# Expert weights of a Mamba and mixture-of-experts layer: one run of memory per partition and transfer, and down weights in two transfers

## The reference, cut to what matters

```
xn = layernorm(x)                                    # [2048, 512]
out = x + mamba(xn) + moe(xn) + shared(xn)

# mamba: in_proj to 2 x 1024 channels, a causal convolution of 4 taps, x_proj to dt, B and C,
#        a scan over 2048 tokens with 16 states per channel, gate, out_proj
# moe:   64 experts, 6 per token, at most 64 tokens per expert
buf = xn gathered by expert                          # [64, 64, 512]
g = einsum('ech,ehi->eci', buf, w_gate)              # w_gate, w_up: [64, 512, 352]
u = einsum('ech,ehi->eci', buf, w_up)
y = einsum('eci,eih->ech', silu(g) * u, w_down)      # w_down: [64, 352, 512]
# each y is weighted by its score and added to its token
# shared: the same form with 704 hidden channels, for all tokens
```

## Time and profile before

| what | value |
|---|---|
| time, 3 runs | 1358.88, 1363.42, 1363.46 us; median 1363.42 |
| profiled execution: span from first to last instruction | 1386.3 us |
| profiled execution: time around the span | none is given; the span is all that the profile shows of it |
| TensorE / VectorE / ScalarE / GpSimd busy | 1291.9 / 1095.9 / 910.5 / 878.1 us |
| DMA moved | 304.82 MB in 129710 packets, mean 220 GB/s |
| w_gate, w_up | 32 transfers each of 1408 KB |
| w_down | 66 transfers of 512 KB and 33 of 384 KB |

### The profile page before, as it was taken

How to read it: one execution, slowest core, us unless ns; L and a number is a source line. 1 busy time by engine, 2 the same in 40 slices (tenths; PEclk the granted TensorE clock), 3 DMA queues, 4 the chain that set the end, 5 groups by cost and what they waited for, 6 DMA issues and landing times.

```text
span 1386.3 us, 53429 instructions
## 1 busy us (share of the span) xinstructions
PE 1291.9 (93%) x21591; PEld 808.3 (58%) x21591; DVE 1095.9 (79%) x1257; ACT 910.5 (66%) x1914; POOL 878.1 (63%) x522
## 2 busy tenths in 40 slices
PE   4999989699999999999999999999999899999998
PEld 3767767445555545555555555545554577787876
DVE  4798989878988889888888898888898655646554
ACT  3756567478788788887887888777777343434343
POOL 2455448268888988988889889889898421303030
PEclk9999999789999999999999999999999999999999
DMA  8153534859898998998989989989889761313130
GB/s 289 65 224 118 218 120 172 272 170 297 257 295 274 283 269 257 304 280 248 306 259 279 288 248 308 285 252 290 263 255 300 243 231 51 132 45 137 37 144 30
DMA packets 129710, 304.82 MB, mean 220 GB/s; under 512 B 18512, under 2 KB 20304, under 8 KB 127824
## 3 DMA queue, kind: packets, MB, share of 16 engines
q1 hardware_dynamic: 122048, 285.13, 63.3%
q0 software_dynamic: 7600, 18.91, 6.0%
HBM read 213.91 MB, written 56.77 MB: 195 GB/s over the span
## 4 chain that ended last, share of the span: by engine, by line
PE 61%; DVE 11%; issue 6%; DVEq 1%; DMA 1%; ACT 0%; POOL 0%; ACTq 0%; POOLq 0%
PE p_dBx L1313 18%; PE p_y L1322 9%; DVE state L1002 8%; PE p_dBx L1372 7%; PE p_g L1299 6%; PE p_g L1282 6%; PE p_dt L1262 2%; PE p_y L1383 2%; PE p_g L1383 2%; PE p_u L1383 2%; PE p_dt L1383 2%; PE p_u L1268 2%; DVE out_operand_parts L1037 2%; PE p_u L1289 1%; PE p_u L1282 1%
## 5 line engine op out<-in xcount | busy, mean ns | idle before, releaser
L1002 DVE TENSOR_TENSOR_SCAN state<-dA,state_carry,p_dBx 128x512 f32<-128x512 f32 x512 | 626.9, 1266 | 104.3 <-PE p_dBx L1313 96.8
L937 POOL TENSOR_TENSOR h_times_C<-state,C_bcast 128x1024 f32<-128x1024 f32 x128 | 307.1, 2400 | 87.4 <-DVE state L1002 86.6
L1313 PE MATMUL p_dBx<-B_diagonals,step_rows 64*32 64x128 f32 x16384 | 327.9, 275 | 30.0 <-issue 20.4
L1313 PEld LDWEIGHTS p_dBx<-B_diagonals,step_rows 64*32 64x32 f32 x16384 | 242.3, 106 | 178.8 <-issue 176.8
L937 POOL TENSOR_TENSOR C_bcast<-state,C_bcast 128x1024 f32<-128x1024 f32 x128 | 319.9, 2787 | 18.1 <-DVE state L1002 18.1
L1152 ACT ACTIVATE dA<-dt_blocks_odd,A_par 128x512 f32<-128x512 f32 x256 | 169.7, 710 | 14.8 <-DMA dt_blocks_odd<-step_rows 14.8
L1152 ACT ACTIVATE dA<-dt_blocks_even,A_par 128x512 f32<-128x512 f32 x256 | 169.7, 710 | 4.2 <-DMA dt_blocks_even<-step_rows 4.2
L276 POOL TENSOR_TENSOR w_in_parts_lo<-C_bcast,w_in_parts_hi 128x512 fp32r<-128x512 f32 x64 | 89.8, 1406 | 113.0 <-ACT w_in_parts_hi L485 112.8
L952 POOL TENSOR_TENSOR step_rows<-step_rows 128x512 f32<-128x512 f32 x16 | 21.9, 1401 | 182.3 <-DMA step_rows<-moe 182.3
L364 DVE SCALAR_TENSOR_TENSOR conv_out<-conv_in,conv_w,conv_out 128x512 f32<-128x512 f32 x96 | 100.4, 1055 | 10.3 <-ACT conv_out L499 8.0
L1299 PE MATMUL p_g<-w_down_pair,step_rows 128*64 128x512 f32 (+1 forms) x396 | 92.3, 601 | 0.0
(11 more groups left out here) (184 smaller groups left out, 2111.1 us busy)
## 6 DMA issues: line engine op xcount, KB each, us to landing
w_gate_pair<-in_w_gate SPq DMA_DIRECT2D x32, 1408.0 KB
w_up_pair<-in_w_up SPq DMA_DIRECT2D x32, 1408.0 KB, 8.0
w_down_pair<-in_w_down SPq DMA_DIRECT2D x66, 512.0 KB
dt_blocks_odd<-step_rows SPq DMA_DIRECT2D x256, 64.0 KB
dt_blocks_even<-step_rows SPq DMA_DIRECT2D x240, 64.0 KB
w_down_pair<-in_w_down SPq DMA_DIRECT2D x33, 384.0 KB
g_d<-y_gated SPq DMA_DIRECT2D x33, 256.0 KB, 4.8
sz_d<-silu_gate SPq DMA_DIRECT2D x32, 256.0 KB, 2.0
```

What stands on the lines that cost most here:

```text
L937: pool.tensor_tensor(hc[m][:, b, :, :], hb[:, q, :, :], Cb[:, NM * cp + GS * m:NM * cp + GS * m + GS, :], ALU.mult).then_inc(s_hc, 1)
L1002: ins = dve.tensor_tensor_scan(hb[:, g % NBUF, s, :], dA[:, g % NBUF, s, :], pB[:, g % 2, :].rearrange("p (t s) -> p s t", s=GS)[:, s, :], ...
L1313: ins = pe.matmul(out[DB * p:DB * p + DB, half, j, :, :], dtxT[k, j * P + DB * b:j * P + DB * b + DB], diag[k, ND * cp + 2 * j + p // 2, a ...
```

## The change

The host lays w_gate and w_up out as [pair, partition, expert, 4, 352], so that what one partition receives is one run of 11264 bytes; `load_gate` and `load_up` are still one transfer each. The buffer of w_down has its dimensions swapped, from [partition, expert, block, 512] to [partition, block, expert, 512], and its weights are stored in two arrays. The first, `w_down`, has for partitions 0 to 95 the rows of all three blocks and both experts, 12288 bytes in one run. The second, `w_down_rest`, has for partitions 96 to 127 the rows of the first two blocks, 8192 bytes in one run. Both are loaded with one transfer each. `down` waits for a count of 32 per pair in place of 48. What is computed stays the same, in the same order.

```diff
-        wd = sb("w_down_pair", [P, 2, len(IK), H])
+        wd = sb("w_down_pair", [P, len(IK), 2, H])
...
-        swd = wd[:, :, :, :].rearrange("p a m h -> p (a m) h")
+        swd = wd[:, :, :, :].rearrange("p m a h -> p (m a) h")
...
             def load_wd(i):
-                for m, (at, k) in enumerate(IK):
-                    sp.dma_start(wd[0:k, :, m, :], io["w_down"][i][:, at:at + k, :].rearrange("a p h -> p a h")).then_inc(s_wd, 16)
+                tail = IK[-1][1]
+                sp.dma_start(wd[0:tail, :, :, :], io["w_down"][i]).then_inc(s_wd, 16)
+                sp.dma_start(wd[tail:P, 0:len(IK) - 1, :, :], io["w_down_rest"][i]).then_inc(s_wd, 16)
...
-                pe.wait_ge(s_wd, 16 * len(IK) * (n + 1))
+                pe.wait_ge(s_wd, 32 * (n + 1))
...
-                        ins = pe.matmul(pG[r, :], hT[0:k, m, r], wd[0:k, a, m, :], start=m == 0, stop=m == len(IK) - 1)
+                        ins = pe.matmul(pG[r, :], hT[0:k, m, r], wd[0:k, m, a, :], start=m == 0, stop=m == len(IK) - 1)
...
-        sp.dma_start(self.wg[:, :, :, :], self.io["w_gate"].rearrange("n a (p k) i -> n p a k i", k=KH)[i]).then_inc(self.s_wg, 16)
+        sp.dma_start(self.wg[:, :, :, :], self.io["w_gate"][i]).then_inc(self.s_wg, 16)
...
-        sp.dma_start(self.wu[:, :, :, :], self.io["w_up"].rearrange("n a (p k) i -> n p a k i", k=KH)[i]).then_inc(self.s_wu, 16)
+        sp.dma_start(self.wu[:, :, :, :], self.io["w_up"][i]).then_inc(self.s_wu, 16)
...
+    pair_rows = lambda a: pairs(a).reshape(NP, 2, P, KH, I).transpose(0, 2, 1, 3, 4)
+    down = pairs(v["w_down"])
+    down = np.concatenate([down[:1], down])
+    tail = IK[-1][1]
+    down_all = np.stack([down[:, :, at:at + tail] for at, _ in IK], axis=1).transpose(0, 3, 1, 2, 4)
+    down_rest = np.stack([down[:, :, at + tail:at + P] for at, _ in IK[:-1]], axis=1).transpose(0, 3, 1, 2, 4)
...
-        "w_gate": pairs(v["w_gate"]), "w_up": pairs(v["w_up"]),
-        "w_down": np.concatenate([pairs(v["w_down"])[:1], pairs(v["w_down"])]),
+        "w_gate": pair_rows(v["w_gate"]), "w_up": pair_rows(v["w_up"]),
+        "w_down": down_all, "w_down_rest": down_rest,
```

## The result

The changed kernel takes 1382.41 us at the median of 4 runs (1378.07 to 1388.86), the kernel before 1362.85 (1358.88 to 1363.46) beside it: a ratio of 1.013, 95% interval 1.0094 to 1.0166 (estimated from all the runs; the quotient of the two medians is 1.0144). That is **slower**, and above the range of the prediction.

A forecast was written before the change was run, and what follows sets the result against it. The prediction took TensorE's products and VectorE's scan, not DMA, to bound the loop. Its terms, 0 + 0 + 0 + 1.0 + 0 = +1.0 us, carried over to the median of 1363.42, gave 1364.4 us, range 1358 to 1368.

The forecast's parts named there:

- Part 1: Gate and up weights in one run per partition: 1.44 MB take 3.4 us either way, saving 0.
- Part 2: w_down in two transfers: 5.8 us of DMA time, 1.6 us more per step, hidden, cost on the path 0.
- Part 3: One SyncE issue less per step: about 0.5 us, which only lengthens SyncE's wait ahead of load_dt, saving 0.
- part 5: End of the loop: the backlog behind the last w_down ends 1.6 us later, by about 1107, cost 0.
- cover: Idle DMA time while SyncE issues dt's spreads: 2.3 us in four, taking up the added 1.6 us per step.
- Steps stay: Sign to check in the loop: steps stay at 24.7 to 25.1 us; wrong if they change by over 0.2 us.
- The chain stays free of DMA: Sign to check in the loop: no transfer appears in the chain between 300 and 1080 us.
- Part 4: Start of the loop: the first gather, moving among w_down's packets, ends +1.0 us later, up to 3.2 us.
- That rise moves along, and I price nothing for it: After the first gather: TensorE's clock rise from 1.2 to 2.4 GHz shifts with it, no cost beyond the shift.
- B: Rival: a step's first dt block reaches ScalarE too late, +12 to +31 us, 1375 to 1394; chance 0.08.
- A: Rival: long runs bring w_down to 428 GB/s and ScalarE's waits shrink, 1355.3 to 1356.5; chance 0.06.
- C: Rival: transfers are cut into the same packets as now, so the layout does nothing, 1363.4; chance 0.03.

The follow-up runs named there:

- e2: The changed kernel with w_down loaded as before, so only the gate and up layout is new: 1367.31 us, ratio 0.9998 to the kernel before.
- e12: The changed kernel, unedited, run again on a chip with the longer step: 1398.95 us, ratio 1.0082 to the kernel before.
- e3: The changed kernel with w_gate and w_up loaded as before, so only w_down is new: 1391.12 us, ratio 1.0185 to the kernel before.
- e8: The changed kernel with the first w_down issued only after the first gather has landed: 1385.06 us, ratio 1.0124 to the kernel before.
- e5: The changed kernel with w_down's rows set apart in DRAM, so its packets stay 2048 bytes: 1393.42 us, ratio 1.0178 to the kernel before.
- e6: The changed kernel with w_down zero-padded into one transfer of 128 partitions, 12288 bytes each: 1359.51 us, ratio 0.9953 to the kernel before.
- e13: The kernel of e6, unedited, run again on a chip with the longer step: 1387.63 us, ratio 0.9984 to the kernel before.
- e4: The changed kernel with w_down cut by blocks, 128 rows of 8192 bytes, then 96 of 4096: 1363.63 us, ratio 0.9987 to the kernel before.

## Why the prediction was wrong

**Right.** Part 1 held (e2, 1.0). Part 2's DMA time held: 5.8 us forecast, 6.0 by the measured rates, the 96-row rate 253 forecast and 250 measured; the row of 253 GB/s did speak against the change. Part 3 held in its effect, though SyncE's wait at load_dt grew by 20 us (43.8 to 64.2), not 14; part 5 shows no loss. Packets: 102510 forecast, 101981 counted; of the 529 that are missing, 528 are under 512 bytes. The ordinary step stayed in place as forecast in the two traces of the changed kernel (after and e12): the waits for dt of ScalarE rose (to 82.6 and 49.8 us, where 30 to 50 were forecast) and were absorbed ahead of VectorE's scan.

**The step that failed** is in part 2, "Does +1.6 us reach anyone?", with its answer "Cost on the path: 0". The runs show about 18 us in its place. I had priced 51 us for no cover at all, but gave that no chance, and had no rival for a cover that holds in most steps and fails in some. It failed in three ways.

*The list of customers.* I listed whoever reads a transfer that the kernel issues: the down product, the gate product, dt. Two that suffer were not on it: x for VectorE's `dt_x` (3.8 to 23.0 us of waiting), and code for TensorE at the changes of chunk. The second makes the loop's loss in the two traces of the changed kernel, where the long steps grow by 9.7 us and on the other chip by 6.9. In the traces of slower executions of kernels that cut the rows as it does, the ordinary steps grow by more than the long ones: 16.0 against 7.8 us in e3, 19.1 against 9.1 in e8, 24.4 against 12.0 in e5, and there x and dt come late enough to reach TensorE. I had seen none of it because I read only the chain and steps around 350, 760 and 1106 us; the long steps (26.7, 26.8 and 27.7) were in the trace of before and would have shown where the engines have nothing spare.

*The cover.* It was judged from one gap of 4 us at a share of 0.43. The mean share over the loop, 0.91, left 2.2 us per step of 24.9, of which 1.6 were to go. On the chips that give 1363 to 1367 us a step is 1 us shorter with the same bytes, the share is 0.94, and 1.4 us are left in 23.9: less than the change adds. The sign was on the page: I wrote down that the span stood 22.9 us above the median, and carried the difference over as a constant, in place of asking what in the loop was 1 us shorter in those runs. A smaller cover there fits the larger loss, 1.3 to 1.9% (changed kernel and e3) against 0.8% on the other kind of chip, though no run varied it alone.

*The sign I trusted.* "Steps stay" was right for 29 steps and said nothing of 3. "The chain stays free of DMA" failed by its own test: x holds 9.55 us of the changed kernel's chain at 956.34, and 10.49 at 972.13 in e12. Nor was it a sharp sign, since the scatter holds 5.18 us of the chain of the kernel before, run again.

**Part 4** was mis-sized: +1.0 us taken, up to 3.2 as the bound, and 3.8 measured (2.5 to 3.8 in the kernels with 96 and 32 rows and long runs, against runs of before on the same kind of chip; 1.7 with e5's short runs). The bound came nearer than the value I chose, which had no row of its own behind it, but its mechanism, each of the gather's 5 packets per engine waiting behind one long run of w_down, is not borne out by itself: with runs of the same length but all 128 rows the gather takes 0.7 us more in e6 and 0.5 less in e13, and with e4's 8192 and 4096 bytes it takes what it took before (7.90). It is again the cut into 96 and 32 rows that costs, and with it the length of the runs (1.7 us with short ones, 2.5 and more with long ones). "That rise moves along, and I price nothing for it" failed too: TensorE stood still longer and ran at 1.2 GHz longer, 1.4 us.

**The rivals.** B had the right sign, and its place was wrong: the 96-row rate did not halve, and in the changed kernel's traces VectorE's scan waits no longer for `dA` than before. Slower executions bear B out in part: in e5's step from 411.9 us the first dt block lets ScalarE start 7.37 us late, ScalarE's copy behind it (L1117) is late too, and TensorE waits 2.06 us for that. "Large pieces keep small transfers behind them waiting" was its argument and points the right way, for pieces of code and of x more than of dt, though the size of the pieces decides little: e5's short ones lose as much. A and C fell. By the ratio the loss is about 18 us (19.6 between the medians), where the profiled executions differ by 11; the traces of e3, e5 and e8 suggest that the rest is ordinary steps of 26 us and more in slower executions, but no slower execution of the changed kernel itself was profiled on that kind of chip.

**Open.** Why one chip has steps of 24.9 us and another 23.9, for the kernel before alike; the first kind shows TensorE's short "issue" waits at dB*x 43 to 48 times, the second 4 to 7 times. Those waits differ by 15.6 us between the two traces of before (19.9 and 4.3), of 26 us in the medians; what makes them wasn't tried. How much of the grown ordinary steps is x and how much dt isn't separated. e3 loses more than the changed kernel (1.0185 and 1.013, with intervals that overlap); whether longer gate and up runs help once the engines are full was not settled, since e12 ran on the other kind of chip.

## What to carry to other kernels

Before packing a load into fewer, longer runs, ask which partitions each transfer covers: 128 rows padded with zeros moved faster (429 GB/s) than exact rows cut into 96 and 32 (250 and 205). When the DMA share is near 0.9 or above, some DMA time added anywhere is paid where the schedule has no slack, so read the longest steps, not the typical one, and count the engines' own code fetches and VectorE's small inputs among the customers. Here the code of a hardware loop was fetched around its first pass, so that pass is where to look. And if the traced execution stands apart from the median of the runs, find what differs before pricing a cover on it.

## What was not expected of the hardware

- TensorE's gaps for "issue" at a change of chunk grow with the DMA load beside them: 2.5 to 3.1 us per long step at a share of 0.94, 3.9 to 5.8 at 0.99. All 54 of over 1 us in the loop, in 17 traces, end 1.2 to 1.7 us after a 16 KB instruction packet has landed.
- The length of the runs matters little from 2048 bytes up: 392 to 429 GB/s for 128 rows; for 96 rows 225 and 253 at 2048 bytes, 288 at 4096, 250 at 12288.
- The same program has two step lengths on different chips, 2% apart, and the same change costs 0.8% on one and 1.3% on the other.
